# Next rows' load and last result's store, moved from the convolution to the landmark heads

## The reference

```python
# a) non-local block ("the convolution")
theta, phi, g = xf @ W_theta + b_theta, xf @ W_phi + b_phi, xf @ W_g + b_g      # 256 -> 32
x = x + (softmax(theta @ phi.T) @ g) @ W_out + b_out
# b) Nystrom attention, 8 heads of 32, 128 landmarks, on layer_norm(t)
q_l, k_l = means of q and k over groups of 8 tokens
kernel_1, kernel_2, kernel_3 = softmax(q k_l'), softmax(q_l k_l'), softmax(q_l k')
pinv = kernel_2's inverse by 6 steps  A_k @ (2 I - A @ A_k)
t = t + (kernel_1 @ (pinv @ (kernel_3 @ v))) @ w_out.T + b_out
# c) mixture of experts on layer_norm(t): 16 experts, top 2, 256 -> 512 -> 256, gelu
t = t + sum over the 2 chosen experts of gate * (gelu(xf @ W1e) @ W2e)
```

## Time and profile before

| | before |
|---|---|
| median of 3 runs | 961.38 us (960.09 to 963.8) |
| the profiled execution's own time | 967.43 us |
| its span, first to last instruction | 965.7 us |
| mean granted TensorE clock | 0.964 of full |
| TensorE busy | 893.0 us (92%) |
| VectorE busy | 541.8 us (56%) |
| ScalarE busy | 439.9 us (46%) |
| GpSimd busy | 367.0 us (38%) |
| the 4 passes | 0 to about 650 us |
| the experts' blocks | from about 650 us on |

### The profile page before, as it was taken

One profiled execution on the slowest core, in us unless ns is written; L12 is line 12 of the kernel. 1 busy time (PEld: TensorE's weight loads), 2 busy tenths in 40 slices (PEclk: granted clock), 3 DMA queues, 4 the chain that ended last, 5 costly groups with the idle time before them and its releaser, 6 DMA issues.

```text
span 965.7 us, 20967 instructions
## 1 busy us (share of the span) xinstructions
PE 893.0 (92%) x6617; PEld 682.4 (71%) x6618; DVE 541.8 (56%) x1585; ACT 439.9 (46%) x981; POOL 367.0 (38%) x457
## 2 busy tenths in 40 slices
PE   6999989889999999998988999989999999999994
PEld 4565767556776656676755667679899998889983
DVE  4477757588675768774748877564562222222220
ACT  3434358433347542436743334763544444344431
POOL 3150003042322215222304032353777665666754
PEclk9599999899999989999979999999999999999998
DMA  3100000300000120000040201668544443334330
GB/s 120 44 2 1 2 1 24 108 3 1 1 2 1 44 89 1 1 2 1 24 153 4 86 2 8 216 204 261 77 71 77 69 66 62 56 58 64 61 53 3
DMA packets 49772, 51.23 MB, mean 53 GB/s; under 512 B 12833, under 2 KB 42913, under 8 KB 49697
## 3 DMA queue, kind: packets, MB, share of 16 engines
q0 software_dynamic: 16768, 19.01, 12.4%
q1 hardware_dynamic: 30608, 31.11, 10.0%
q10 hardware_dynamic: 2320, 0.14, 0.2%
HBM read 33.13 MB, written 19.06 MB: 54 GB/s over the span
## 4 chain that ended last, share of the span: by engine, by line
PE 67%; DVE 12%; DMA 7%; issue 7%; ACT 2%; POOL 2%; SPq 1%; ACTq 0%; POOLq 0%; DVEq 0%
PE PS L726 11%; PE PS L1196 9%; PE PS L1207 9%; PE PS L1096 8%; PE PS L758 7%; DMA out_dram<-low,row_of 5%; PE PS L826 3%; PE PS L837 3%; PE PS L929 3%; PE PS L831 3%; DVE neg_max L1454 3%; PE PS L908 3%; PE PS L913 1%; PE PS L1024 1%; DMA low<-rows_scratch,token_of 1%
## 5 line engine op out<-in xcount | busy, mean ns | idle before, releaser
L1454 DVE TENSOR_REDUCE neg_max<-PS 128x1 f32<-128x1024 f32 (+1 forms) x96 | 117.4, 1222 | 94.2 <-PE PS L837 34.3
L564 POOL DMA_INDIRECT out_dram<-low,row_of x79 | 125.3, 1586 | 90.4 <-SPq L708 42.8
L726 PE MATMUL PS<-ident,arena 128*128 128x128 f32 x1008 | 142.8, 289 | 14.4 <-ACT arena L1324 7.8
L1196 PE MATMUL PS<-low 128*128 128x128 f32 x1264 | 154.1, 275 | 0.0
L726 PEld LDWEIGHTS PS<-ident,arena 128*128 128x128 f32 x1008 | 123.3, 151 | 42.3 <-issue 33.1
L1207 PE MATMUL PS<-arena,low 128*128 x632 | 149.4, 380 | 0.2 <-issue 0.2
L2079 DVE TENSOR_SCALAR low<-PS,slot_gate 128x256 f32<-128x256 f32 x79 | 38.2, 484 | 197.8 <-PE PS L1207 137.0
L1196 PEld LDWEIGHTS PS<-low 128*128 128x128 f32 x1264 | 147.5, 192 | 0.1
L1324 ACT COPY arena<-PS 128x1024 f32<-128x1024 f32 x96 | 98.4, 1025 | 90.8 <-PE PS L726 90.7
L1207 PEld LDWEIGHTS PS<-arena,low 128*128 128x128 f32 x632 | 114.1, 190 | 12.7 <-issue 0.4
L1392 ACT ACTIVATE low<-PS 128x512 f32<-128x512 f32 x79 | 47.2, 597 | 154.0 <-PE PS L1196 154.0
(11 more groups left out here) (278 smaller groups left out, 1341.6 us busy)
## 6 DMA issues: line engine op xcount, KB each, us to landing
arena<-in_L_ffn_W_dram SPq DMA_DIRECT2D x32, 512.0 KB, 6.6
out_dram<-t SPq DMA_DIRECT2D x4, 1024.0 KB, 9.2
arena<-in_x_dram SPq DMA_DIRECT2D x3, 1024.0 KB, 6.5
rows_scratch<-arena SPq DMA_DIRECT2D x4, 512.0 KB, 3.6
rows_scratch<-arena SPq DMA_DIRECT2D x8, 256.0 KB, 2.6
low<-rows_scratch,token_of POOLq DMA_INDIRECT x79, 2.9
out_dram<-low,row_of POOLq DMA_INDIRECT x79, 3.8
arena<-in_x_dram SPq DMA_DIRECT2D x2, 512.0 KB, 4.7
```

The lines of the kernel that those rows point to most:

```text
L564: pool.indirect_dma_start(out_rows, bass.IndirectOffsetOnAxis(ap=row_of[:, n:n + 1], axis=0), y_sb[:, n % 4, :], None, bounds_check=T - 1, ...
L726: mm = pe.transpose(PS[0:s.shape[1], dst_bank, n * P:n * P + s.shape[0]], s, ident[0:s.shape[0], 0:s.shape[0]])
L1196: mm = pe.matmul(PS[:, 2 + p, hc * P:(hc + 1) * P], w1_now[:, p, c * H + hc * P:c * H + (hc + 1) * P], xgT[:, p, c, :], start=c == 0, stop ...
L1454: dve.tensor_reduce(dst, src, AX.X, ALU.max, negate=True).then_inc(s_max, 1)
```

## The change

SyncE waits longer in passes 0 to 2: for the scores of unit NT + 1 (head 1, counting heads from 0) ahead of the load, and, in passes 1 and 2, for those of unit NT + 3 (head 3) ahead of the store. No instruction is added or taken away elsewhere, and the order of the DMAs on SyncE stays as it was. Pass 3 is not touched.

```diff
@@ -637,8 +637,10 @@
                 sp.wait_ge(x_loaded, (i + 1) * 16)
                 sp.wait_ge(bulk_mm, mm_count(i, UNIT_ORDER[0]) - 1)
                 sp.wait_ge(xb_ready, i + 1)
+                sp.wait_ge(s_mm, i * UNITS + NT + 2)
                 load_x(i + 1)
                 if i >= 1:
+                    sp.wait_ge(s_mm, i * UNITS + NT + 4)
                     store_out(i - 1)
                 for first, last in ((0, 4), (4, 6), (6, NT)):
                     store_rows(i, first, last)
```

## The result

The changed kernel takes 979.8 us in the median of four runs (970.9 to 985.0), beside 961.5 us of the kernel before on the same chip (960.1 to 963.8): a ratio of 1.0178 with a 95% interval of 1.0093 to 1.0263. It is slower by 17 us (9 to 25). Its four runs lie 14 us apart, those of the kernel before 4 us, and no run here shows why. The forecast was 976.4 us, slower by 15.0, in a range of 967 to 983.

A forecast was written before the change was run, and what follows sets the result against it. TensorE was taken to bound the kernel, with the VectorE steps it waits for. Stalls of 11.55 us plus 3.4 us of half clock made 15.0 us on the 961.4 us median, forecasting 976.4 us, range 967 to 983.

The forecast's parts named there:

- Which resource decides: Moved load and store cost nothing; GpSimd's 4.52 us sum, which waits for the load, delays VectorE steps TensorE needs.
- When the sum starts: Load lands 5.6 us after issue behind head 1's scores; GpSimd's sum starts at 85.73 (pass 0) and 239.93 (pass 1).
- rival (a): Load lands after 6.5 us, so line 1849 or the cast of 1672 is held instead; 14.0 us, 975.4; chance 0.15.
- The store's term: Store held until head 3's scores still finishes before the third stage overwrites its tile, 40 us to spare; priced at nothing.
- Whether the step is held: In the landmark heads, VectorE's line 1846, a 128x8 two-SBUF-operand product, is blocked until GpSimd's sum ends.
- rival (c): VectorE steps this small slip past GpSimd's sum, or GpSimd yields: no stall, 961.4 us, no change; chance 0.12.
- Rival (b): Only single-operand copies and scalings are held, two-operand steps pass; 7.85 us, 9.5 with one clock fall, 971; chance 0.08.
- The size of the stalls: VectorE's held step in the heads delays passes 0 to 2 by 3.15, 4.2 and 4.2 us, together 11.55 us.
- The clock: TensorE's half-clock spell after idling costs 1.7 us a fall, added in passes 0 and 2: 3.4 us.
- The upper bound that I kept: Clock term's upper bound, 8.5 us: spells twice as long, 3.4 us in passes 0 and 2, 1.7 more in pass 1.
- Rival (d): Faster: without transfers each convolution's opening half-clock spell ends one step sooner, some 5 us saved, 956; chance 0.05.

The follow-up runs named there:

- e2: Changed kernel with the load's wait removed, so only the store is moved into the landmark heads; 963.6 us, ratio 1.0002.
- e8: Changed kernel, both transfers moved, with GpSimd's sum of input and bias put behind its cell scatters, waiting for the scores of head 7; 961.7 us, ratio 0.9996.
- e11: Changed kernel, both transfers moved, with GpSimd's sum between the scatters of heads 3 and 4 (pass 0: after head 3's scores); 962.3 us, ratio 0.9983.
- e4: Kernel before, transfers left in the convolution; only GpSimd's sum in passes 0 to 2 waits for TensorE's second norm product; 978.4 us, ratio 1.0137.
- e1: Changed kernel with the store's own wait removed, so only the load is moved to the landmark heads; 976.1 us, ratio 1.0103.
- e3: Changed kernel, both transfers moved, with GpSimd's sum waiting for the scores of head 3; 972.8 us, ratio 1.0086.
- e6: Kernel before with one wait changed: GpSimd's bias add to row tile 6 comes only after VectorE's norm of row tile 7; 959.9 us, ratio 0.9978.
- e9: Kernel before, transfers left in the convolution, with GpSimd's sum waiting for the scores of head 3; 975.8 us, ratio 1.0151.
- e10: Kernel before, transfers and sum left in place; only GpSimd's cell scatters wait for the scores of head 4; 979.2 us, ratio 1.0152.
- e5: Changed kernel with GpSimd's sum cut into 8 instructions of 256 columns; 968.3 us, ratio 1.0068.
- e7: Changed kernel plus unused TensorE transposes in passes 0 to 2: 10 ahead of line 1087, and 4, 8 and 8 ahead of line 1091; 974.9 us, ratio 1.0123.

## Why the prediction was right, and where it was off

**Which resource decides.** Right. The argument was that the transfers are free on both sides and that their follower on GpSimd is what counts. e2 (store alone, 1.0002), e8 and e11 (both transfers moved, the sum elsewhere, 0.9996 and 0.9983) and e4 (nothing but the sum moved, 1.0137) bear it out together.

**When the sum starts.** Right in two passes of three. I took 5.6 us from the issue to the landing, as in the earlier trace rows; the sum started after 5.56, 5.52 and 6.75 us. The third is rival (a)'s landing, and there rival (a)'s victim was held, the cast. I had given (a) 0.15 as a case for all passes; the landing differs from pass to pass, and in e1 two other steps were victims, each in one pass. The price hardly depends on it, as its sum of 14.0 us against 15.0 said. The store's term, nothing, was right.

**Whether the step is held.** Right, and rival (c) falls: line 1846, a product of two SBUF tiles of eight columns, which no row showed held, was blocked to the end of the sum. That is what the Trainium skill states (SBUF — State Buffer, Who interferes with whom). The trace agrees: 4.19 us in place of 0.17, for the whole rest of the GpSimd instruction. Line 1614, which the prediction set beside that statement, has one SBUF tensor as its input and so was no test of it. Rival (b) falls with it, since it let such products pass, though its own class, a scaling from SBUF to SBUF, is held as well (e1, 3.77 us).

**The size of the stalls.** 3.15, 4.2 and 4.2 us forecast, 2.90, 4.01 and 4.07 measured, 11.0 in place of 11.55 us. Most of the small difference is the end: I had it 0.15 us behind the sum, from the earlier trace rows, and it was 0.02 to 0.03 us.

**The clock.** This term was too small for the changed kernel: 3.4 us forecast, 7.0 us in its trace. Two choices account for it. I took the price of a fall from pass 1 of the earlier trace rows, 1.7 us, where TensorE had idled for 1.03 us and the spell lasted 3.4 us. The spells after the long stalls of the changed kernel last 6.8 us and cost (2.08 − 1.16) + (3.62 − 1.88) + (1.3 to 1.4 − 1.05), up to 3.0 us each. And I counted pass 1 as paid already because before fell there. It was not: by the longer spell it lost 1.3 us more. Nor does that fall belong to pass 1. Of the eight profiles that leave the small steps alone, before and e3 have one such fall in pass 1, e2 and e6 have one in pass 2, and e8 to e11 have none, all with the same 1.03 to 1.04 us of idling in front.

The upper bound that I kept, 8.5 us for spells twice as long, was the right picture for this trace: 3 × 3.0 − 1.7 = 7.3 us, and 961.4 + 11.0 + 7.3 = 979.7 us, with 979.8 measured. That this is so close is partly luck, since the measurement has 8 us to either side. The same mechanism cost less in e1 and e4: 10 and 13 us by their ratios, with clock terms of 4.5 and 4.0 us in their profiles, nearer to the 3.4 of the forecast. In pass 2 of e1 an idle time of 4.63 us was followed by the short spell. With some 11 us of held time the three profiles make 14.5 to 18 us, and the three ratios give 10, 13 and 17. The idle times were shorter than the 5 to 6 us of the forecast: 3.9, 4.8 and 5.1 us in passes 0 to 2 of the changed kernel.

**Rival (d).** Wrong in its premise as the earlier trace rows said. Without transfers the convolution's opening is neither shorter nor longer in a pattern. In pass 1 its first spell at half clock lasts 6.8, 3.4, 3.4 and 10.2 us in before, e4, e9 and e10, which have the transfers there, and 13.7, 3.4, 10.2 and 10.2 us in the changed kernel, e1, e8 and e11, which don't.

**What I hadn't thought of.** That holding back the same GpSimd work past the small steps isn't free as such. For the change itself this cost nothing, but the remedy that the theory suggested first, e3, gave back only half of the loss.

## What to carry to other kernels

When a transfer is moved, ask what waits for its landing and what that follower shares with the engines at its new place. Here 1 MB moved either way costs nothing, and one 4.5 us GpSimd instruction behind it costs 10 to 17 us, because it lay beside VectorE steps of two to sixteen columns that TensorE waits for. A stall of TensorE costs its length and, on top, the half-clock spell behind it, here 4 to 7 us over three stalls. Give that price as a range, and don't count a fall in one profiled execution as a fall in all. If the follower must be there, put it beside VectorE steps that read PSUM (e8, e11), which is worth more than cutting it into pieces (e5). Look too at what queues behind it: e3 and e9 put it there with a wait that also held up the scatters, and were slow.

## What the runs showed of the hardware that I hadn't expected

- A held VectorE step ends 0.02 to 0.03 us behind the 4.5 us GpSimd instruction, and its own size doesn't matter: two columns, eight or sixteen all took 3.8 to 4.5 us. Held were products of two SBUF tiles, a cast to int32 and a scaling; not held were reductions and copies out of PSUM (1.23 and 0.28 us in e8), a sum with one operand in PSUM (0.68 us) and reciprocals of one column (0.15 us).
- An idle time of 1.99 us ahead of line 1091 (e5, pass 1) was followed by the same half-clock products, 2.08 and 3.62 us, as one of 5.10 us (pass 2 of the changed kernel). One of 1.03 us was followed by none in most passes and by a spell of 3.4 us in four. Halving a stall did not halve the clock's part.
- VectorE can wait 2 to 8 us for TensorE's results with nothing in the trace that explains it (e3, e5, e7, e9, e10), for which no cause was found.
